# Three edits of order in a four-layer graph network on one Trainium2 core: where the first outputs, the layer-2 bias and the last normalisations are computed

## The reference

```python
# layers 0, 1, 2: attention
h = x @ W                       # layer 2: + W_b
e = leaky_relu(s_left[i] + s_right[j])          # s = h @ a, slope 0.2
e = where(adj > 0, e, very_negative)
alpha = softmax(e)              # layers 0, 2 over j; layer 1 over i
out = alpha @ h                 # layers 1, 2: elu(out)
# layer 3: relations
out = sum_r (adj == r) @ x @ weight[r] + bias
# after every layer
x = layernorm(x + out)
```

## Time and profile before

| | us |
|---|---|
| median of three runs | 422.62 (421.92 to 424.2) |
| the profiled execution, its own time | 422.4 |
| span of its trace, first to last instruction | 420.6 |

### The profile page before, as it was taken

The page is one execution under the profiler, slowest core; times in us unless marked ns, Lnnn a source line. Parts: engine busy times, 40 slices in busy tenths (PEclk is TensorE's granted clock), DMA queues, the critical chain, the costliest instruction groups (busy, mean ns, idle before and its releaser), DMA issues. The chain is left out here.

```text
span 420.6 us, 9211 instructions
## 1 busy us (share of the span) xinstructions
PE 359.4 (85%) x2786; PEld 317.4 (75%) x2793; DVE 362.7 (86%) x1390; ACT 309.6 (74%) x832; POOL 296.5 (70%) x367
## 2 busy tenths in 40 slices
PE   7888999999969687786877899999998779899970
PEld 6778999999968686785877789898898765555550
DVE  0655999999999999999999988998998997899982
ACT  2775999999765767755867777677786737888865
POOL 5365789777776774665574676777777856899994
PEclk8998999999989999999899999999999999999995
DMA  6999953000000000000000000000000000012122
GB/s 171 213 247 247 247 105 52 2 1 2 2 1 2 1 2 1 2 2 1 2 1 2 1 2 2 2 1 2 0 2 3 0 2 1 2 75 79 75 77 104
DMA packets 8756, 18.20 MB, mean 43 GB/s; under 512 B 1280, under 2 KB 2560, under 8 KB 8704
## 3 DMA queue, kind: packets, MB, share of 16 engines
q0 software_dynamic: 2304, 8.39, 10.6%
q1 hardware_dynamic: 5280, 8.72, 5.9%
q10 hardware_dynamic: 1120, 0.46, 0.5%
HBM read 21.76 MB, written 4.19 MB: 62 GB/s over the span
## 5 line engine op out<-in xcount | busy, mean ns | idle before, releaser
L531 PE MATMUL o_ps<-h_scaled,PT 128*128 128x129 f32 (+1 forms) x1536 | 185.5, 280 | 5.3 <-DVE PT L1015 2.7
L531 PEld LDWEIGHTS o_ps<-h_scaled,PT 128*128 128x128 f32 x1536 | 180.1, 196 | 7.3 <-issue 3.3
L1015 DVE SCALAR_TENSOR_TENSOR PT<-rows_ps,factors,MT 128x512 f32<-128x512 f32 x128 | 88.7, 736 | 0.0
L770 ACT ACTIVATE X<-y,rstd 128x128 f32<-128x128 f32 x192 | 61.0, 389 | 31.9 <-POOL rstd L298 31.9
L298 POOL TENSOR_TENSOR rstd<-var_eps,neg_half 128x4 f32<-128x4 f32 x64 | 70.0, 1094 | 5.0
L468 PE MATMUL h_ps<-wx,xT 128*128 128x130 f32 x384 | 53.3, 282 | 23.0 <-DVE smax L964 20.8
L468 PEld LDWEIGHTS h_ps<-wx,xT 128*128 128x128 f32 x384 | 47.9, 192 | 28.7 <-issue 28.5
L1091 DVE BATCH_NORM_STATS2 stats<-y 128x6 f32<-128x128 f32 x256 | 56.0, 280 | 6.7 <-DVE y L1071 0.5
L248 POOL TENSOR_TENSOR mean_term<-h_mean,empty_row 128x512 f32<-128x512 f32 x32 | 38.2, 1193 | 17.5 <-DVE residual L1071 14.2
L313 POOL TENSOR_TENSOR elu_exp<-elu_exp,X 128x512 f32<-128x512 f32 x32 | 40.7, 1273 | 7.5 <-ACT elu_exp L763 7.2
L272 POOL TENSOR_TENSOR h_scaled<-hx,factors 128x516 f32<-128x516 f32 x32 | 35.0, 1095 | 12.5 <-PE o_ps L531 8.4
(11 more groups left out here) (119 smaller groups left out, 659.2 us busy)
## 6 DMA issues: line engine op xcount, KB each, us to landing
MT<-adj_by_j POOLq DMA_DIRECT2D x16, 512.0 KB, 13.4
X<-x SPq DMA_DIRECT2D x16, 256.0 KB, 8.2
out<-X SPq DMA_DIRECT2D x16, 256.0 KB, 2.0
w_rel<-w SPq DMA_DIRECT2D x1, 256.0 KB, 4.6
w_back<-w_by_output ACTq DMA_DIRECT2D x1, 192.0 KB, 3.2
wx<-w_by_input ACTq DMA_DIRECT2D x1, 192.0 KB, 3.7
bias<-b ACTq DMA_DIRECT2D x1, 64.0 KB, 3.0
bias<-b SPq DMA_DIRECT2D x1, 64.0 KB, 4.7
```

The source lines that it names most:

```text
L531: last = pe.matmul(o_ps[it.b][:, ic, first:1 + D], PT[:, it.b, jc, ic * P:(ic + 1) * P], h_scaled[:, it.b, jc, first:1 + D], start=(jc == ...
L770: last = act.activation(X[:, it.g, c, :], y[:, it.b, c, :], ACT.Copy, scale=rstd[:, it.b, c:c + 1])
L1015: dve.scalar_tensor_tensor(out=PT[:, it.b, c, :], in0=rows_ps[:], scalar=factors[:, it.b, 1, c:c + 1], in1=m, op0=ALU.max, op1=ALU.mult, * ...
```

## The change

There are three edits. In the diff below, `split_bias2` belongs to GpSimd, the first `attention_slot` to TensorE, `take_bias2` to ScalarE, `normalize_last` and the second `attention_slot` to VectorE.

1. Up to slot 3 (the new constant `TURN`), VectorE runs `take_out` of item `n-2` as the first step of its slot instead of after the maximum and the row factors. In slot 3 TensorE now spreads the rows, then the maximum, and then transposes; before, it transposed first, then did the maximum and then the rows. `project` and `attend` stay behind these in slot 3.
2. The five GpSimd steps of the layer-2 bias run one a slot, in slots 20 to 24, ahead of `scale_h`; the nine ScalarE steps run three a slot, in slots 25, 26 and 27, ahead of `take_scaled`. TensorE waits for three increments instead of one.
3. For graphs 14 and 15 of layer 3, GpSimd no longer computes `offset` and ScalarE no longer normalises. VectorE does it, one slot earlier in the loop (`normalize_last`), as four `tensor_scalar` instructions that subtract the mean and multiply by `rstd`; SyncE waits for VectorE's semaphore for these two outputs.

```diff
+FIRST_ON_VECTOR = G - 2
+BIAS_SLOT = G + 4
+TURN = LAST_EARLY + 1
...
-                sp.wait_ge(sem("x_new"), it.done)
+                if it.g < FIRST_ON_VECTOR:
+                    sp.wait_ge(sem("x_new"), it.done)
+                else:
+                    sp.wait_ge(sem("x_last"), it.g + 1 - FIRST_ON_VECTOR)
...
-            def split_bias2():
+            def split_bias2(n):
...
+                if n == BIAS_SLOT + 1:
+                    pool.wait_ge(sem("bias2"), 1)
+                    pool.tensor_copy(bias2_hi[:, :], bias2[:, :]).then_inc(sem("bias2"), 1)
...
                     find_rstd(at(-2))
+                split_bias2(n)
                 if at(1) and at(1).l == 1:
                     scale_h(at(1))
-                if n == G + 8:
-                    split_bias2()
...
                     find_rstd(at(-1))
-                    find_offset(at(-1))
+                    if at(-1).g < FIRST_ON_VECTOR:
+                        find_offset(at(-1))
...
-                    pe.wait_ge(sem("bias2_parts"), 1)
+                    pe.wait_ge(sem("bias2_parts"), 3)
...
             def attention_slot(at, n):
-                if n > LAST_EARLY:
+                if n > TURN:
                     next_transpose_of(at)
-                if at(2) and n > LAST_EARLY:
+                if at(2) and n > TURN:
                     spread_max(at(2))
                 if at(1):
                     spread_rows(at(1))
-                if at(2) and n <= LAST_EARLY:
+                if at(2) and n <= TURN:
                     spread_max(at(2))
-                if n < 0:
+                if n < 0 or n == TURN:
                     next_transpose_of(at)
...
+            def take_bias2(n):
+                for k, part in enumerate((bias2_hi, bias2_mid, bias2_low)):
+                    if n == BIAS_SLOT + 5 + k:
+                        act.wait_ge(sem("bias2"), 5)
+                        row = slice(32 * k, 32 * k + 1)
+                        act.copy(bias2_parts[row, 0:130], part[row, :])
+                        act.copy(bias2_parts[row, 130:260], part[row, :])
+                        act.activation(bias2_parts[row, 260:260 + D], part[row, 0:D], ACT.Copy, scale=float(N))\
+                            .then_inc(sem("bias2_parts"), 1)
...
                     take_next(at)
+                take_bias2(n)
                 if at(-3) and at(-3).l != 1:
                     take_scaled(at(-3))
...
-                if n == G + 10:
...
-                if at(-3):
+                if at(-3) and at(-3).g < FIRST_ON_VECTOR:
                     take_norm(at(-3))
...
+            def normalize_last(it):
+                dve.wait_ge(sem("rstd"), it.done)
+                dve.wait_ge(sem("mean_var"), it.done)
+                for c in range(C):
+                    last = dve.tensor_scalar(X[:, it.g, c, :], y[:, it.t, c, :], mean_var[:, it.t, c, 0:1],
+                                             rstd[:, it.t, c:c + 1], ALU.subtract, ALU.mult)
+                last.then_inc(sem("x_last"), 1)
             def attention_slot(at, n):
+                if at(-2) and n <= TURN:
+                    take_out(at(-2))
                 if at(-1) and at(-1).l in (0, 2):
                     row_sums(at(-1))
...
-                if at(-2) and at(-2).l == 0:
+                if at(-2) and at(-2).l == 0 and n > TURN:
                     take_out(at(-2))
...
                     aggregate(at(-1))
+                if at(-2) and at(-2).g >= FIRST_ON_VECTOR:
+                    normalize_last(at(-2))
```

More of the change, by code:

```diff
@@ L314, in elu_low @@
                     .then_inc(sem("elu_low"), 1)
-            def split_bias2():
[L318 to L330, removed]
+            def split_bias2(n):
+                if n == BIAS_SLOT:
+                    pool.wait_ge(sem("b2_a"), 1)
+                    pool.wait_ge(sem("b_in"), B_IN)
+                    pool.tensor_tensor(bias2[:, D:D + 2], b2_a[:, :], ab2_sb[:, :], ALU.add).then_inc(sem("bias2"), 1)
+                if n == BIAS_SLOT + 1:
+                    pool.wait_ge(sem("bias2"), 1)
+                    pool.tensor_copy(bias2_hi[:, :], bias2[:, :]).then_inc(sem("bias2"), 1)
+                if n == BIAS_SLOT + 2:
+                    pool.wait_ge(sem("bias2"), 2)
+                    pool.tensor_tensor(bias2_rest[:, :], bias2[:, :], bias2_hi[:, :], ALU.subtract)\
+                        .then_inc(sem("bias2"), 1)
+                if n == BIAS_SLOT + 3:
+                    pool.wait_ge(sem("bias2"), 3)
+                    pool.tensor_copy(bias2_mid[:, :], bias2_rest[:, :]).then_inc(sem("bias2"), 1)
+                if n == BIAS_SLOT + 4:
+                    pool.wait_ge(sem("bias2"), 4)
+                    pool.tensor_tensor(bias2_low[:, :], bias2_rest[:, :], bias2_mid[:, :], ALU.subtract)\
+                        .then_inc(sem("bias2"), 1)
             def attention_slot(at, n):
```

## The result

| | median us | ratio to before, 95% interval |
|---|---|---|
| before (4 runs beside it) | 423.41 (421.92 to 424.35) | |
| the changed kernel (4 runs) | 419.23 (417.43 to 419.98) | 0.9913 [0.9884, 0.9943] |

The kernel is faster by 3.7 us, with an interval from 2.4 to 4.9. (Ratios, intervals and gains are estimated over all runs of both kernels, so a gain need not be the difference of the two medians beside it.) The forecast was 416.1, with a range up to 418.7: the direction was right, the size was not. The profiled execution took 419.3 us and its span is 417.1; before they were 422.4 and 420.6.

What follows compares the result with a forecast made beforehand. No engine's total decides; waits between engines in layer 0, bias slots in layer 1 and the closing chain do. 422.4 − 2.7 (first `y`) − 2.1 (bias) − 1.5 (last graphs) = 416.1 us; range 414.8 to 418.7, own range 415.0 to 417.4.

Steps and rivals of the forecast that it cites:

- The output transfers and what follows keep their 3.6 us: Kernel's end: from the last normalisation's end at 417.0 to the span's end at 420.6, 3.6 us, was to stay the same.
- the terms of the 1.5: Last two graphs: normalisation ends at 414.3 + 0.3 + 0.05 + 0.85 = 415.5 instead of 417.0; bounds 0.8 and 2.0 us.
- the forecast gave 0.3 away: Graph 15: GpSimd's `var_eps` can lose up to 0.54 us beside VectorE's graph 14 instructions; 0.3 us was taken.
- it had 0.85: Graph 15: VectorE's four instructions after `rstd` were to take 0.85 us, with 0.9 and 1.13 as bounds.
- I take 1.71: Layer 0, slot 2: with TensorE's pause halved, its clock holds and `attend` of graph 2 gains 1.71 us; bounds nothing or 1.71.
- Rival (b): Layer 0, slot 2: the clock falls all the same, edit 1 gives 1.0 us, total 417.8; chance 0.12.
- The base: The gains were subtracted from the profiled execution's 422.4 us, 0.2 under the median.
- against 2.1: Layer 1's bias steps, moved to where GpSimd and ScalarE wait, were to gain 2.1 us; bounds 0.0 and 2.2.
- Rival (c): VectorE and GpSimd hold each other up: edit 2 gives 0.3, edit 3 0.8 us, total 418.6; chance 0.10.
- The wait of edit 1: Layer 0, slot 2: with `y` first, `attend` of graph 2 starts at 30.6 instead of 31.52, 0.9 us gained.
- Its reorder: Layer 0, slot 3: both reorderings take `own_max` to `attend` from 3.32 to 3.2 us, counted as 0.1 us.
- (d): Layer 0's transfers set the time, edit 1's shift is lost, only 1.5 us stay: 420.9; chance 0.08.

## Why the prediction was wrong

- **Edit 3, "The output transfers and what follows keep their 3.6 us": this step failed.** The 1.5 us up to the last write came as worked out (1.52). What follows took 4.7, because the engine that writes last is now one with whose closing branch an instruction fetch comes, and that fetch lies in the way of one sixteenth of the last output. I had looked at what each engine computes at the end, not at what its queue does after it. Moved, the branch gives the 1.1 us of the wait back (418.0, inside the forecast's range), and moved in the kernel before, it takes 0.9 [0.0, 1.7].
- **Edit 3, the terms of the 1.5: luck in part.** `var_eps` and `rstd` of graph 15 lost nothing beside VectorE's first four instructions (0.20 and 1.01 us), where the forecast gave 0.3 away; and VectorE's four instructions took 1.11 us (graph 15's, from 411.29), where it had 0.85. The two errors are of one size and cancel.
- **Edit 1, "I take 1.71": mis-sized.** The mechanism was right: `attend` at 3.81 us, no fall in any of nine traces, 2.72 us in the trace against 2.7. But the 1.71 us was one execution's. The kernel before has executions without that fall, and they lose about 1 us at the start in its place. Counted in full it gave 2.7; measured alone the edit gives 1.7 [0.9, 2.6]. By the traces, five parts in seven of 2.72 and two of 1.15 make 2.3, which is inside. With the start counted in, slot 4's maximum stands at 46.3 us after the span's start on the mean of those seven traces and at 44.7 on that of the nine: 1.7 us. Rival (b) had a fall that stays; what happened is a fall that sometimes was not there.
- **The base.** The sum was made against an execution of 422.4. The median of the kernel before is 423.0 to 423.4 over more runs, so 416.1 is 416.7 against that.
- **Edit 2: right, a little too high.** 1.6 [0.7, 2.5] against 2.1. From the first reciprocal of layer 1 to the last, the nine traces with edit 2 take 114.93 to 116.38 us, mean 115.5, the nine without it 116.99 to 117.98, mean 117.3: 1.8 us. Rival (c), VectorE and GpSimd holding each other up, showed in one step of five, as 0.24 us; in the nine traces it hits at most one step each, and two of them not at all.
- **The wait of edit 1: right**, 0.88 us less pause against 0.9. Its reorder, forecast at 0.1, is too small to tell.
- **Rivals.** (d) did not come: from 30 to 120 us one pause of a computing engine is ended by a transfer, GpSimd's 0.17 us in slot 3, and it stands in the kernel before as well. Of (c), the hold on graph 15's `rstd` did not come either. (e) did not come: falls of the clock in layer 1 are in the traces on both sides, and by the spread above they cost at most 1.5 us of the layer.

The miss of 3.1 us is thus 0.6 of base, 1.1 of fetch (shown both ways), 0.4 of a fall counted in full and 0.3 of edit 2 (both from means over traces), and a rest of 0.7. The starts are of that size: slot 1 ends at 29.6 us on the mean of the seven traces with the old order and at 30.1 on that of the nine with the new. But the starts of one program lie 0.7 us (changed kernel) to 1.0 us (kernel before) apart, so whether this is chance or comes with the change stays open; it is inside the intervals of the runs, which are about ±1 us each.

## What to carry to other kernels

When work is moved to another engine at the very end, follow that engine's queue past its last instruction: a fetch that comes with its closing branch can delay the last output, so let that engine wait for the output before it branches. (Here this was tried for VectorE alone.) A stall that you price from one trace, above all one of the clock, needs a second trace of the same program before it is counted in full. And an expected gain that is exact in the trace but missing in the median is a reason to look at the parts of the kernel that the change does not touch.

## What the runs showed of the hardware

- With an 8 KB instruction fetch of 0.31 us among an output's last packets, one sixteenth of that output landed 1.1 us late, though the other fifteen parts were not touched; with the fetch gone, all sixteen landed together.
- One and the same program started with TensorE's clock in different places: slot 1 ended at 29.17 or 30.15 us. The whole took 422.4 or 422.9 us: the quick start lost its lead in slot 2 (slot 4's maximum at 46.39 or 45.88), and layer 1 took 116.99 or 117.73.
- At the start the record of the granted clock reads 1.00 while four transposes take 1.11 us in place of 0.66 (first of the two later executions of the kernel before, 7.33 to 8.44): there the durations have to be read, and not the record.
- The mean granted clock does not rank kernels: the one with the five matmuls in the pause has 0.967 against 0.971 and is 1.7 us faster.
